# Five stages of a graph network's first layer become one pass over chunks of five node tiles, and the gated mix's second norm becomes one factor for each node

## The reference, cut to what matters

```
xn = layernorm(x)
agg = segment_sum(softmax_by_dst(q[src] . k[dst]) * v[src], dst)
skip = xn @ Wskip.T + bskip
g    = sigmoid(concat([skip, agg, skip - agg]) @ Wgate.T + bgate)
rst  = prelu(layernorm(g * skip + (1 - g) * agg) * ln_w + ln_b)
# mix
out  = q @ context                         # q = xn @ Wq, context from exp(k), v
gate = sigmoid(gelu((layernorm(xn) * ln_g + ln_b) @ Wg1 + bg1) @ Wg2 + bg2)
mix  = (out * gate) @ Wproj + bproj
x = x + rst + mix
# eight soft experts
n = layernorm(x);  w = softmax(n @ Wr + br)
y_e = relu(bn2(relu(bn1(n @ W1_e)) @ W2_e)) @ Wo_e + bo_e
x = x + sum_e w_e * y_e
# second layer: edge convolution
h = layernorm(x) @ W_node.T + b_node
msg = (edge_attr @ W_edge.T + b_edge) * h[src]
```

## Time and profile before

| what | value |
|---|---|
| median of 3 runs | 3904.84 us (3903.76 to 3905.72) |
| the profiled execution's own time | 3902.24 us |
| its span | 3900.5 us |
| TensorE busy | 3041.8 us (78%) |
| VectorE busy | 2121.6 us (54%) |
| ScalarE, GpSimd busy | 1171.5 us (30%), 1107.6 us (28%) |
| mean granted TensorE clock | 0.891 |

### The profile page before, as it was taken

The page is one execution under the profiler, slowest core; times in us unless marked ns, Lnnn a source line. Parts: engine busy times, 40 slices in busy tenths (PEclk is TensorE's granted clock), DMA queues, the critical chain, the costliest instruction groups (busy, mean ns, idle before and its releaser), DMA issues. The chain is left out here.

```text
span 3900.5 us, 63882 instructions
## 1 busy us (share of the span) xinstructions
PE 3041.8 (78%) x12424; PEld 2266.2 (58%) x12425; DVE 2121.6 (54%) x3774; ACT 1171.5 (30%) x2667; POOL 1107.6 (28%) x1235
## 2 busy tenths in 40 slices
PE   3766666388867338999997999999977877657979
PEld 2644433255554334676776888888866755544568
DVE  6377777778732861111114555555548865883231
ACT  1000000078634112333331000000019965653312
POOL 3177777211100000000002555555530003640023
PEclk9877878699988757999998999999988988988979
DMA  1599999477600000000003665556540000004244
GB/s 56 197 300 315 314 315 315 152 207 201 178 1 19 0 17 0 16 8 16 8 0 123 174 180 174 177 175 176 176 139 0 1 20 0 1 1 169 81 138 139
DMA packets 224195, 456.10 MB, mean 117 GB/s; under 512 B 30330, under 2 KB 113730, under 8 KB 222714
## 3 DMA queue, kind: packets, MB, share of 16 engines
q1 hardware_dynamic: 163066, 262.12, 21.6%
q0 software_dynamic: 61056, 193.06, 15.7%
HBM read 365.75 MB, written 90.31 MB: 117 GB/s over the span
## 5 line engine op out<-in xcount | busy, mean ns | idle before, releaser
L1446 POOL DMA_INDIRECT conv_h<-table_h,conv_ix x424 | 409.2, 965 | 1049.5 <-ACT conv_ix L1437 963.0
L1497 PE MATMUL bank<-conv_w,conv_eT 128*128 128x256 f32 x2532 | 581.4, 379 | 0.0
L1497 PEld LDWEIGHTS bank<-conv_w,conv_eT 128*128 128x128 f32 x2532 | 482.2, 190 | 65.1
L519 PE MATMUL bank<-scores_k,scores_hotT 128*128 x864 | 325.2, 513 | 150.6 <-DVE scores_hotT L549 147.1
L497 POOL DMA_INDIRECT x<-table_qv,scores_ix x324 | 306.4, 946 | 244.0 <-ACT scores_ix L487 161.9
L519 PEld LDWEIGHTS bank<-scores_k,scores_hotT 128*128 128x128 f32 x864 | 192.7, 247 | 253.3 <-issue 229.8
L1396 DVE SCALAR_TENSOR_TENSOR x<-bank,soft_w,x 128x256 f32 x200 | 96.8, 484 | 443.3 <-PE bank L1330 443.3
L1358 ACT ACTIVATE soft_h<-bank,soft_bi,soft_sc 128x320 f32<-128x320 f32 x320 | 197.5, 617 | 340.0 <-PE bank L1323 340.0
L908 PE MATMUL bank<-attend_pv,attend_hot 128*128 128x260 f32 x848 | 237.2, 405 | 55.0 <-POOL attend_pv L842 30.7
L1437 ACT ACTIVATE conv_ix<-src 128x2 int32 x212 | 43.2, 204 | 770.8 <-DVE conv_msg L1471 737.8
L1504 PE MATMUL bank<-conv_msg,conv_hot 128*128 128x256 f32 x848 | 223.2, 386 | 43.6 <-DVE conv_msg L1471 43.6
(11 more groups left out here) (421 smaller groups left out, 5380.4 us busy)
## 6 DMA issues: line engine op xcount, KB each, us to landing
conv_eT<-in_edges SPq DMA_DIRECT2D x212, 384.0 KB, 3.2
attend_v<-edge_v SPq DMA_DIRECT2D x212, 256.0 KB, 3.0
edge_v<-x SPq DMA_DIRECT2D x162, 256.0 KB, 4.7
edge_v<-scores_qv SPq DMA_DIRECT2D x54, 256.0 KB
hidden_rows<-rows SPq DMA_DIRECT2D x25, 512.0 KB, 3.8
top_wd<-in_top_wd SPq DMA_DIRECT2D x8, 1024.0 KB, 11.6
conv_h<-table_h,conv_ix POOLq DMA_INDIRECT x424, 3.3
x<-in_x SPq DMA_DIRECT2D x2, 3200.0 KB, 13.0
```

What stands on the lines that cost most here:

```text
L519: mm = nc.tensor.matmul(banks[u % UN][:, g * F:(g + 1) * F], hotT[:, u % UN, g * P:(g + 1) * P], k[:, bass.ds(t, 1), :].rearrange("p t f - ...
L1446: nc.gpsimd.indirect_dma_start(out=h[:, u, g, :], out_offset=None, in_=m.d_h, in_offset=bass.IndirectOffsetOnAxis(ap=ix[:, u * G + g:u * G ...
L1497: mm = nc.tensor.matmul(banks[u][:, g * F:(g + 1) * F], eT[:, u, g, c], w[:, c], start=c == 0, stop=c == EC - 1)
```

## The change

`load_small`, the norm of the mix, `first_update`, "norm1", `soft_experts`, "norm2" and the h table are gone. Two functions take their place, both without loops in the program: every instruction is written out.

*The mix.* A normalised row that is normalised again is the row times one factor. `layer_norm` keeps the variance in `m.twice` (one copy), `linear_attention` makes the factor of it (three small VectorE operations, a square root on ScalarE, a reciprocal). The gain goes into `wg1`, the shift into a bias row `b1`, and Wq times context is made once as `wqc`. The mix then runs over chunks of 640 nodes, with hidden products of chunk `ch`, their turn for `ch - 1` and the gated products for `ch - 2` in one round. `linear_attention` also loads all small weights of later stages and saves the step table to HBM, since `m.steps` and `m.node_no` now share an area with the node stage's buffers.

*The node stage.* `node_layers` makes rounds c = -1 to 5. In a round, chunk p = c + 1 goes through update, norm 1 and router, chunk x = c through the eight experts, and chunk q = c - 1 through norm 2 and the h table. The weights of all eight experts are loaded at its start. Hidden groups use three PSUM banks (`HIDS`), outputs two (`OUTS`), side products the other three.

```diff
+    CH = U * P
+    HIDS, OUTS = 3, 2
+    SPARE = HIDS + OUTS
...
+        def rounds():
+
+            for c in range(-1, TU + 1):
+                yield c, c + 1 if c + 1 < TU else None, c if 0 <= c < TU else None, c - 1 if c >= 1 else None
...
+                for e in range(XQ):
+                    for k, x in enumerate(("ffn_w1", "ffn_w2", "ffn_wo")):
+                        sp.dma_start(W[:, e, k], a[x][e]).then_inc(wload[e], 16)
...
             @block.gpsimd
             def _(pool):
-                pool.sem_inc(w_used, 2)
-                nc.gpsimd.memset(m.sums[:], 0.0)
+                for p in range(TU):
+                    nc.gpsimd.tensor_tensor(m.x[:, tiles(p)], m.x[:, tiles(p)], bproj.unsqueeze(1).to_broadcast([P, U, F]), ALU.add).then_inc(x_biased, 1)
+                for p in range(TU):
+                    pool.wait_ge(var_a, p + 1)
+                    nc.gpsimd.memset(m.sums[:, tiles(p)], 0.0)
...
+                def expert(c, e):
+                    n = c * XQ + e
+                    if c == 0:
+                        pe.wait_ge(wload[e], 48)
+                    if e == 0:
+                        pe.wait_ge(kept_b, 3 * c + 3)
...
+                                if k >= HIDS:
+                                    pe.wait_ge(relu, k - HIDS + 1)
...
+                        if k >= OUTS:
+                            pe.wait_ge(summed, k - OUTS + 1)
...
+                for c, p, x, q in rounds():
+                    for e in range(XQ):
+                        if x is not None:
+                            expert(x, e)
+                        if e == 0 and p is not None:
+                            take(skip_kept, p + 1)
+                            rows_of(lambda u, f: m.xT[:, f, p * CH + u * P:p * CH + (u + 1) * P], m.wskip, skipped)
+                        if e == 1 and p is not None:
+                            take(proj_kept, p + 1)
+                            rows_of(lambda u, f: m.mixed[:, p, f, u * P:(u + 1) * P], m.wproj, projected)
...
+                        if e == 7 and x is not None:
+                            take(biased, x + 1)
+                            for u in range(U):
+                                mm = nc.tensor.matmul(half(u), wT[:, u * P:(u + 1) * P], bo[:], start=True, stop=True)
+                            mm.then_inc(turned_w, 1)
...
+                                for u in range(U):
+                                    c_(nc.vector.scalar_tensor_tensor(junk[:], res[:, u], 1.0, gate_res, ALU.mult, ALU.mult,
+                                                                      accum_out=dots[:, 1, u:u + 1]))
...
+                        if x is not None:
+                            for u in range(U):
+                                k = (x * XQ + e) * U + u
+                                dve.wait_ge(outs, k + 1)
...
+                nc.gpsimd.iota(m.node_no[:], [[1, NP]], base=0, channel_multiplier=0,
+                               allow_small_or_imprecise_dtypes=True).then_inc(numbered, 1)
...
-        layer_norm(nc, "norm0", m.x, m.rows, m.xT, m.ident, banks)
+        layer_norm(nc, "norm0", m.x, m.rows, m.xT, m.ident, banks, m.twice)
```

More of the change, by code:

```diff
@@ L130, in mean_and_variance, with layer_norm @@
     c(nc.vector.tensor_scalar(mv[:, :, 1], mv[:, :, 1], LN_EPS, None, ALU.add))
[L133 removed]
+def layer_norm(nc, name, src, rows, cols, ident, banks, spread=None):
     with Stage(nc, name) as st:
@@ L1074, in _ @@
+                for ch in range(TU + 2):
+                    if ch < TU:
+                        hide(ch)
+                    if 0 <= ch - 1 < TU:
+                        turn(ch - 1)
+                    if ch >= 2:
+                        products(ch - 2)
             @block.scalar
             def _(act):
-                act.wait_ge(loaded, 80)
-                act.sem_inc(gelu, 2)
-                act.sem_inc(sig, FT)
-                with act.Fori(0, NC // 2) as ii:
-                    for u in range(2):
-                        act.wait_ge(hid, ii * 2 + u + 1)
-                        nc.scalar.activation(hT[:, bass.ds((ii * 2 + u) * CW, CW)], banks[u][0:GH, 0:CW], ACT.Gelu,
-                                             bias=bg1[:]).then_inc(gelu, 1)
@@ L1084, in _ @@
-                with act.Fori(0, NC) as i:
-                    for c in range(FT):
-                        act.wait_ge(product, i * 6 + 3 + c)
-                        act.wait_ge(mixed, i * FT + c + 1)
-                        nc.scalar.activation(gate[:, c], banks[4 + c][:, 0:CW], ACT.Sigmoid, bias=bg2[:, c:c + 1]).then_inc(sig, 1)
+                for f in range(FT):
+                    act.wait_ge(folded, f + 1)
+                    nc.scalar.activation(wqc[:, f], banks[5 + f][:, 0:F], ACT.Copy).then_inc(wq_kept, 1)
@@ new lines, in node_layers, with chunk, columns @@
+        rstd = st.sb("rstd", [P, 3, U])
+        work = st.sb("work", [P, U])
+        def chunk(at):
+            return flat[:, at:at + U * F].rearrange("p (t f) -> p t f", f=F)
+        def columns(at):
+            return flat[:, at:at + U * F].rearrange("p (f n) -> p f n", f=FT)
+        skip, hrow = chunk(0), chunk(U * F)
+        res = chunk(steps_at)
+        h1, h2 = columns(steps_at + U * F), columns(steps_at + 2 * U * F)
+        bskip, ln_w, ln_b, bproj, gate_skip, gate_res, gate_both, bnode = (m.vec[:, k] for k in range(8))
@@ new lines, in rows_of, with turn @@
+                def rows_of(src, weight, sem):
+                    for u in range(U):
+                        for f in range(FT):
+                            mm = nc.tensor.matmul(half(u), src(u, f), weight[:, f], start=f == 0, stop=f == FT - 1)
+                    mm.then_inc(sem, 1)
+                def turn(rows, sem):
+                    for u in range(U):
+                        for f in range(FT):
+                            tr = nc.tensor.transpose(half(u)[:, f * P:(f + 1) * P], rows(u)[:, f * P:(f + 1) * P], m.ident[:])
+                    tr.then_inc(sem, 1)
```

713 lines of the change are left out of this document (395 added, 318 removed).

## The result

The changed kernel takes 3720.44 us (median of four runs, 3712.93 to 3723.99) beside 3904.63 for the kernel before: ratio 0.9524, 95% interval 0.9512 to 0.9535. The forecast was 3720. The total hit closer than its parts did, which the stages show, so part of the hit is luck.

What follows compares the result with a forecast made beforehand. Only the experts' stretch was taken as TensorE-bound, with TensorE mostly waiting around it. Node stage 144 + norm 32.4 + mix 11 − small costs 3 = 184.4 us off 3904.8 gives 3720; range 3685 to 3765.

Steps and rivals of the forecast that it cites:

- The overlap: Node stage: neighbouring chunks' update, router, norm and h table lie beside the experts; with fill and tail, 144 us less.
- two-bank wait: Experts: with two output banks, outputs three and five each wait; outputs take 4.72 us in place of 4.32.
- Slot 0: VectorE's work before the first expert's sums in a round: 10.8 us against 9.9 of cover, 0.8 late, three times.
- The fill: Node stage before its first expert matmul: an uncovered serial chain of 49.4 us plus 9.7 of contention, 59.1 us.
- The contention term: In the fill, GpSimd's five bias additions hold up VectorE's batch norm constants: 9.7 us, bounds 0 and 16.
- The tail: Node stage after the last expert output: uncovered sums, norm, transposes, h products and store, 27.5 us.
- The mix: Mix stage: 59.3 us in place of 70.3, table loads stretching chunks to 11.3; gain 11, bounds 0 and 18.
- small costs: Exp table load behind its wait 1.3 us, semaphore clearing 1.2, iota refilling node_no 0.5: together 3 us lost.
- less waits: Rival: GpSimd's bias does not hold VectorE up (9.7 us) and two output banks suffice (17): 3693 us; chance 0.15.
- slower VectorE slots: Rival: VectorE's slots in the node stage cost half as much again, 34 us more, 3754 us; chance 0.14.
- the unrolled code: Node stage's 2,680 matmul records without loops: charged nothing; rival, not fed at matmul rate, slower than before, chance 0.03.
- the overlap happened: Rival denied here: a wait puts the next chunk's update behind the experts, only 40 us gained, 3864 us; chance 0.02.

Runs made afterwards that it cites:

- serial_rounds: Changed kernel with each chunk's update, experts and norm with h table following one another, without overlap: 4162.20 us against 4171.20 for the kernel before.
- out_banks3: Changed kernel with two PSUM banks for hidden groups and three for outputs, in place of three and two: 3973.99 us, kernel before 4171.20.
- fill_gap: Changed kernel with five matmuls of zeros behind the context's last product, filling TensorE's wait before the mix: 3711.42 us, kernel before 3902.96.
- wide_between: Changed kernel with 256-column matmuls of zeros between the hidden products of the mix's first two chunks: 3708.44 us, kernel before 3902.96.
- bias_late: Changed kernel with GpSimd's projection bias added to later chunks only after the previous chunk's columns are copied: 3965.97 us, kernel before 4171.20.
- mix_gate_pairs: Changed kernel with the mix's two gate products of a half chunk together, then its two attention products: 3963.69 us, kernel before 4171.20.
- sets 0 and 2: Groups of kernels run on one chip beside the kernel before, which took 3904.63 us in set 0 and 3902.96 in set 2.
- unchanged: The changed kernel run once more with nothing altered: 3727.82 us, kernel before 3902.96.
- three_edits: Changed kernel with the edits of bias_late, mix_gate_pairs and out_banks3 together: 3703.32 us, kernel before 3902.96.
- unchanged_2: The changed kernel run again with nothing altered, in another set: 3978.63 us, kernel before 4162.49.

## Why the prediction came out as it did

**The overlap** was right in mechanism and, taken apart, shown by serial_rounds. Rounds of 127.3 us were forecast and two are 127.3, one 126.4; round 0 is 121.8 for 123.6, round 4 is 113.5 for 114.6. Inside a round two terms were off against each other. An expert takes 13.02 us and not 13.25, because the two-bank wait came out at 0.09 us in place of 0.42 (out_banks3): I had taken the first sum to start 1.39 us after its output, and here it starts 1.06 after it. But the first layer of rounds 1 and 2 loses 1.8 us at half clock behind the bias products, which I had not charged. Slot 0, charged with 0.8 us three times, stalls once, by 0.65, in round 3. In rounds 1 and 2 the slow first layer covers it; in fill_gap and wide_between, whose rounds have no half clock, it stalls 0.66 us in each of the three rounds, and with three output banks never. So that term held.

**The fill**: 54.8 us for 59.1. The contention term holds: 9.7 forecast, 9.2 on the constants and 8.4 on the first expert (bias_late). The chain itself is 46.4 and not 49.4: the small operations stand 0.20 us apart where I took 0.23, a dot with its read-out 0.47 where I took 0.52, and the constants take 2.3 where I took 4.0. GpSimd's additions took 2.9 us each and not over 3. The Trainium skill (SBUF — State Buffer, Who interferes with whom) calls the shared port pair an exclusive lock. The constants of 2.4 to 3.0 us beside additions of 2.9 agree with an instruction that waits out a whole addition, and the 4.8 us by the stretch of a single row would have been the wrong number. The first constant, an operation with one tensor as input, was drawn out as well, 1.85 us for 0.18.

**The tail**: 23.8 us for 27.5. ScalarE's root found its table loaded (0.33 us between VectorE's operations, 0.21 of them the root, where I had 1.6), the copies leave TensorE 1.45 us idle in place of 1.9, the h products take 6.5 for 7, and the last store is issued at 1920.71 with the next stage's first load at 1925.10, 4.4 for 5.4.

**The mix** is the term that was wrong in size and in mechanism: 11 us of gain forecast, 0.7 in this trace. Its mechanism was table loads that stretch each chunk to 11.3 us. They did not; TensorE goes through a chunk in 10.75 us without a gap, and ScalarE's loads (1.28 us) fall into its own waits: in the chunk at 1191 it waits 2.67 us for VectorE behind the one and 0.88 and 1.48 for TensorE behind the other. What I lacked is two things. A pair costs 2.01 us and not 1.62, since each change between weights of 64 and of 128 rows leaves 0.2 us open (mix_gate_pairs); over twenty pairs 7.8 us. And the clock: at full clock the mix would be 55 us, better than forecast, but 27 us at half clock cost 14 here and 36 in other executions. I had taken TensorE's clock to be 1.00 wherever it is kept busy. The trace of before already spoke against that: its router products, 100 records of 8 columns, kept TensorE busy for 21.50 of 21.50 us and ran at half clock to their end:

```profile
1430.20:1451.70 21.50, 21.50 (x100) 21.41 (x100) 2.62 (x6) 1.51 (x2) 1.47 (x1) 0.50 0.21 73
```

I had charged this clock to the router in the fill and not asked what it meant for the mix, whose new first layer has narrow records where the old one had streams of 320 columns.

**The norm** (32.4) is right: no instruction of it is left, and the mix's first matmul follows the context's last by 2.5 us.

**The edges** I had held for equal. In the traces of sets 0 and 2 (changed, unchanged, fill_gap, wide_between, three_edits) the context stage begins at 1074.1, 1071.2, 1074.9, 1071.5 and 1077.2 us, in the one trace of before at 1063.1: 8 to 14 us later each time. Most of it is there by 737 us, behind the score stage, where the first matmul of the stage that looks for the largest scores starts at 737.2 and started at 727.9. The code of these stages is the same. From 200 to 700 us the score stage moves 313.2 GB/s in the trace of before and 307.8 to 310.8 in the five others; at 308.8 for 313.2 these 500 us alone would be 7 us longer, by my estimate. Why the rate differs, or whether one trace of before is a fair sample, I did not try apart: this cause is open. So the sum came out by cancelling, which is luck: 184.4 forecast, plus 13.6 in the node stage, less 10.3 in the mix, less 11.0 in the edges, plus 3.2 for small costs that did not come (the context stage is 1.0 longer, what lies behind the node stage 1.2 shorter), is the 180 of the two spans.

The rivals: less waits came half true (two banks suffice, but GpSimd does hold VectorE up), slower VectorE slots did not, the unrolled code is fed at the matmuls' rate (0.216 and 0.269 us a record at full clock), and the overlap happened.

## To carry to other kernels

Serial chains on VectorE that stand between TensorE-bound stages are worth cutting into chunks and laying beside them: here some 40 us of update and 20 of norm per chunk vanish behind 104 of expert matmuls, and only the first and the last are paid. Before that, ask what runs on GpSimd at the moment when VectorE's chain is bare, and move it by one wait. And look at TensorE's granted clock in every stage with narrow streams, in the trace of before already: busy is not enough.

## What the hardware showed that I had not expected

- TensorE stayed at half clock (1.2 GHz) for 56.0 us in which it was busy for 56.0 (unchanged_2), with 64-column records ahead and products of 320 columns under way. Records of 64 columns take 0.11 us each at full clock, those of 256 columns 0.22. With records of 256 columns between them, or 320 in their place, half clock was over within 7 us, four times of four; without, it lasted 14 to 72 us, nine times of nine. Once back, the narrow records of later chunks no longer made it fall. Why the return took 21 us in one execution and 72 in another is open, and so is what the fall itself hangs on: it came behind a wait of 2.5 us in twelve traces, without one in fill_gap, and in the rounds of the changed kernel within 1.1 us behind the bias products, which have 256 columns on eight rows, at two seams of four. At the seams of fill_gap it did not fall, and in mix_gate_pairs it fell once 0.4 us behind the router's products of 8 columns. The Trainium skill (TensorE: Matmul & The Clock Gate, Part 1: The HAM clock gate) says that the gate follows how busy TensorE has been of late. These traces differ: the busy share by itself does not tell the clock here.
- A change between weights of 64 and of 128 rows costs 0.2 us of TensorE (mix_gate_pairs).
- The score stage of one and the same program moved 224 GB/s from 200 to 700 us in unchanged_2 and 311 in unchanged, and the context stage began at 1273.9 and 1071.2 us: 203 us between two chips. The DMA engines were busy for 0.75 of the time in the first and 0.97 in the second, so the slower one was not slow for want of DMA engines; what held it back is open.
